# When ScalarE computes the next batch's sigmoids inside the tiles of the last feed-forward stage

## The reference

```python
    x = x + _L0_attn_ref(_L0_cond_ref(x, fside_BxSxS_0, fside_BxSxS_0, L0_cond_w, L0_cond_u, cond_512), ...)
    x = x + _L0_ffn_ref(_L0_cond2_ref(x, fside_BxSxS_0, ...), ...)      # routed experts
    x = x + _L1_attn_ref(_L1_cond_ref(x, fside_BxSxS_0, ...), ...)      # second layer: state-space block
    x = x + _L1_ffn_ref(_L1_cond2_ref(x, fside_BxSxS_0, ...), ...)      # second layer: feed-forward

        # in _L1_ffn_ref; _mx_linear quantises both of its operands in blocks of 32
        x2d = x.reshape(B * S, H)
        gate = _mx_linear(x2d, gate_w)
        up = _mx_linear(x2d, up_w)
        h = jax.nn.silu(gate) * up
        out = _mx_linear(h, down_w)
```

## Time and profile before

| | |
|---|---|
| median of 3 runs | 4275.18 us (4270.21 to 4276.04) |
| the profiled execution's own time | 4278.56 us |
| its span, first to last instruction | 4276.8 us |
| mean granted TensorE clock | 0.896 of full speed |
| TensorE busy | 3637.4 us, 85% of the span |
| VectorE busy | 2588.9 us, 61% |
| ScalarE busy | 1194.1 us, 28% |
| GpSimd busy | 558.0 us, 13% |

### The profile page before, as it was taken

One profiled execution on the slowest core, in us unless ns is written; L12 is line 12 of the kernel. 1 busy time (PEld: TensorE's weight loads), 2 busy tenths in 40 slices (PEclk: granted clock), 3 DMA queues, 4 the chain that ended last, 5 costly groups with the idle time before them and its releaser, 6 DMA issues.

```text
span 4276.8 us, 38855 instructions
## 1 busy us (share of the span) xinstructions
PE 3637.4 (85%) x13526; PEld 2272.7 (53%) x13526; DVE 2588.9 (61%) x3690; ACT 1194.1 (28%) x1974; POOL 558.0 (13%) x451
## 2 busy tenths in 40 slices
PE   2887887787879999998999779789979898889988
PEld 1653644545537777776776536543654356434743
DVE  5877877877845556776677344564346344644454
ACT  1332332323304444333333222212221222113210
POOL 1003002021021111110111112110212011201100
PEclk9989888889989999999999977899779887998799
DMA  3212202102117667666666510122013201221011
GB/s 142 60 31 61 68 18 74 55 18 72 38 33 258 211 230 236 219 229 197 230 220 226 187 74 30 69 103 79 30 55 117 79 30 54 74 105 48 1 59 40
DMA packets 277843, 444.62 MB, mean 104 GB/s; under 512 B 52560, under 2 KB 189776, under 8 KB 265104
## 3 DMA queue, kind: packets, MB, share of 16 engines
q1 hardware_dynamic: 256768, 383.74, 27.1%
q0 software_dynamic: 20880, 58.40, 4.3%
HBM read 368.49 MB, written 97.70 MB: 109 GB/s over the span
## 4 chain that ended last, share of the span: by engine, by line
PE 59%; DVE 20%; issue 9%; DVEq 5%; ACT 4%; DMA 2%; POOL 1%; POOLq 0%; SPq 0%; ACTq 0%
PE bank L964 14%; PE bank L975 7%; PE bank L1206 5%; PE bank L1219 5%; PE bank L1225 4%; PE bank L782 3%; PE bank L1073 3%; DVE sb_gla L1793 2%; DVE sb_ratio L1768 2%; DVEq L1774 2%; PE bank L1114 2%; PE bank L1092 1%; PE bank L759 1%; DVE sb_work L1805 1%; PE bank L762 1%
## 5 line engine op out<-in xcount | busy, mean ns | idle before, releaser
L964 PE MATMUL bank<-sb_xT,sb_work 128*128 128x256 f32 x3024 | 665.4, 380 | 1.6 <-issue 0.8
L964 PEld LDWEIGHTS bank<-sb_xT,sb_work 128*128 128x128 f32 x3024 | 576.0, 191 | 106.8 <-issue 31.3
L782 PE MATMUL bank<-sb_gla,sb_work 128*128 128x256 f32 x896 | 261.7, 445 | 111.7 <-DVE sb_work L1795 99.1
L975 PE MATMUL bank<-sb_work,sb_hT 128*128 128x512 f32 x756 | 351.0, 616 | 0.0
L1219 PE MATMUL bank<-sb_parts,sb_small 128*128 128x512 f32 x512 | 257.1, 649 | 43.8 <-ACT sb_work L1538 39.0
L782 PEld LDWEIGHTS bank<-sb_gla,sb_work 128*128 128x128 f32 x896 | 189.9, 219 | 174.8 <-DVE sb_work L1795 120.2
L762 PE MATMUL bank<-sb_hT,sb_work 128*128 128x512 f32 x384 | 180.5, 618 | 101.4 <-DVE sb_hT L1742 101.4
L1587 POOL DMA_INDIRECT sb_parts<-scratch_h,sb_small x126 | 136.0, 1079 | 983.3 <-DMA sb_small<-scratch_ids 963.8
L1073 PE MATMUL bank<-sb_parts,sb_hT 128*128 128x512 f32 x512 | 238.6, 627 | 0.0
L1206 PE MATMUL bank<-sb_work,sb_parts 128*128 128x512 f32 x512 | 233.5, 616 | 2.7 <-ACT sb_work L1544 2.7
L975 PEld LDWEIGHTS bank<-sb_work,sb_hT 128*128 128x128 f32 x756 | 145.9, 200 | 161.4 <-issue 161.4
(11 more groups left out here) (363 smaller groups left out, 6113.3 us busy)
## 6 DMA issues: line engine op xcount, KB each, us to landing
sb_work<-scratch_gu SPq DMA_DIRECT2D x63, 1408.0 KB, 7.5
sb_parts<-scratch_mx SPq DMA_DIRECT2D x16, 3072.0 KB, 10.4
sb_work<-moe_w SPq DMA_DIRECT2D x63, 512.0 KB, 5.1
scratch_y<-sb_work SPq DMA_DIRECT2D x63, 512.0 KB, 6.8
sb_parts<-scratch_fq SPq DMA_DIRECT2D x24, 1024.0 KB, 7.9
sb_work<-w_qkvg SPq DMA_DIRECT2D x64, 256.0 KB, 2.6
scratch_gu<-moe_w SPq DMA_DIRECT2D x32, 512.0 KB, 5.8
sb_parts<-fT SPq DMA_DIRECT2D x48, 256.0 KB, 3.7
```

The lines of the kernel that those rows point to most:

```text
L782: mm = pe.matmul(dst.rearrange("p (h n l) -> p h n l", h=HPC, l=size), kS[u % 2][:, k * P:(k + 1) * P], late[:, :, k, :, 1, :], start=True ...
L964: mm = pe.matmul(dst, egu[j % 3][:, which * NC + k, m * P:(m + 1) * P], xt[j % 2][:, k, :], start=(k == 0), stop=(k == NC - 1))
L975: mm = pe.matmul(bank(YB[s]), einter[j % 2][:, m * SLOTS + s * P:m * SLOTS + (s + 1) * P], edn[j % 3][:, m * D:(m + 1) * D], start=(m == 0 ...
```

## The change

In ScalarE's loop over the feed-forward tiles the call of `sigmoid2` moves from the start of the loop's body to its end. The sigmoid of tile `i` then stands behind the activation of tile `i` and behind the copy of tile `i - 1`, where it stood in front of both.

```diff
                 for i in range(FB * NT + 1):
-                    if b + 1 < NB and i >= 8 and i % 2 == 0 and i < 16:
-                        sigmoid2(b + 1, (i - 8) // 2)
                     if i < NT:
                         act.wait_ge(f_tq.sem, f_tq.at(b, i + 1))
...
                         act.activation(hqT[ib % 2][:, :, t * P:(t + 1) * P], r3(bank(6), P), ACT.Copy)\
                            .then_inc(f_hT.sem, 1)
+                    if b + 1 < NB and i >= 8 and i % 2 == 0 and i < 16:
+                        sigmoid2(b + 1, (i - 8) // 2)
```

## The result

| | before | after |
|---|---|---|
| median, four executions of each | 4273.01 us (4270.21 to 4276.04) | 4231.10 us (4221.36 to 4235.63) |
| ratio | | 0.9898, 95% interval 0.9886 to 0.9910 |
| profiled execution | 4278.56 us | 4230.84 us |
| its span | 4276.8 us | 4229.0 us |
| mean granted TensorE clock | 0.896 | 0.904 |

The change makes the kernel 1.0% faster, where 0.8% was forecast: 42 us between the medians and 47.7 us between the profiled executions, against a forecast of 33.3. The fourth execution of the kernel before moved its median from 4275.18 to 4273.01, which is 2.2 us of the 10.8 between the forecast of 4241.9 and the median; the other 8.6 are gain beyond the forecast. The part inside the feed-forward tiles came out as worked out. The rest comes from stretches in which no instruction differs.

The account below looks back on a forecast made before the run. TensorE, busy 85% of the span, was the engine to watch, standing still for late activations. Removed 54.3 us less added 21.0 gave 33.3; 4275.2 - 33.3 = 4241.9 us, range 4236 to 4257 to hold 8 of 10.

Parts of the forecast that it names:

- What goes: Gate products of tiles 9 and 13, six places: activation waits of 40.0 us and slow restarts of 14.3 removed, together 54.3.
- What comes late next: VectorE delays TensorE's up products and transposes at tiles 9 and 13: new waits add 21.0 us in all.
- What the moved sigmoid costs: At its new place behind the copy of tile i - 1: cost 0, upper end 2.4 us.
- The clock at the new waits: TensorE's new waits at tiles 9 and 13: clock fall taken as 0 per place, bounds 0 and 2.97 us.
- The first rival: Clock falls at the six places' new waits all the same: gain 22.3 us, time 4253, upper bound 4260; chance 0.17.
- The rule of the Trainium skill: Short idle times between matmul groups let the clock go down and up; each of the places would keep a slow restart.
- What follows in the batch: Tiles 14 and 15 and the next batch's weights keep their distances and only come earlier, with no further gain.

Follow-up runs that it names:

- even_only: Kernel before with only the sigmoids of tiles 8 and 12 moved to the end of the tile: 4230.28 us, ratio 0.9897.
- odd_only: Kernel before with only the sigmoids of tiles 10 and 14 moved: 4273.36 us beside 4273.47, ratio 1.0001.
- the delays: Transposes of tile 13 done three times over: in the kernel before 4270.12 us, ratio 0.9990; in the changed kernel 4240.93 us, ratio 0.9925.
- the fastest kernel: Changed kernel with VectorE's weighted sums in tiles 4, 5, 8, 9, sigmoids paired, and matmuls of constants filling TensorE's waits: 4190.10 us, ratio 0.9797.

## Why the prediction was right about the change and wrong about the kernel

**What goes** held. The wait for the activation was removed at six places with the slow restart behind it, and even_only and odd_only show that tiles 8 and 12 alone account for it.

**What comes late next** held, with small errors. Tile 9: recorded waits of 1.01 and 1.95 us for 1.36 and 2.00 forecast; tile 13: 1.30 and 1.73 for 1.65 and 2.00. The recorded waits leave out the modelled end of the group before; counted from start to start as in the forecast they are 1.18, 2.22, 1.47 and 2.00, 6.87 us for 7.01. My step of 0.09 us from the sum to the product was wrong: the product started 0.09 us ahead of the sum's recorded end. The sum over the tiles, 33.8 us for 33.3, is right to 2%. One row was misread, with no effect on the sum: 2808.91 is the start of the sigmoid's table load, not its end, which is 2810.19.

**What the moved sigmoid costs**: nothing, as forecast (odd_only, 1.0001).

**The clock at the new waits** held at all six places. After waits of 0.95 to 1.96 us TensorE was not slowed: up products of 3.70 us, transposes of 0.66 us and down products of 13.9. The first rival, a fall at each of the six places, did not occur. That these waits were short enough was a choice between 0 and 2.97 us, with no row to decide it: the choice came true, it was not worked out. The rule of the Trainium skill that the prediction set against it, from "TensorE: Matmul & The Clock Gate", section "A second HAM failure mode: psum-queue depth-cycling", did not hold at these waits between full products; in the state-space stage it does.

**The step that failed** is in the sum: "What follows in the batch (...) keeps its distances and only comes earlier." That put a term at zero. What follows came earlier and was also shorter, by 13.9 us in the profiled execution: 10.7 in the state-space stages of batches 1 to 3 and 3.5 between the last down products and the next batch, less 0.3 elsewhere. I had a wait of 2.67 us before me that lowers the clock, and slow restarts of 5.34 to 6.58 us after waits of nearly one length (6.36 to 6.71 us), which show that the price of a wait is not fixed by its length. I gave the effect some 5 us on either side of zero. The stages above put it at 210.3 to 224.2 us for one batch's state-space stage, so at up to 14 us per batch. My estimate from that is that the range should have been about twice as wide on both sides.

That the sign was a gain here was not to be had from the trace of before. By the delays, another 0.87 us per batch takes 10 us of the gain back. So of the 42 to 48 us measured, 34 belong to the change and the rest, a piece of luck, to where it happened to put the later waits. This last is shown by the trace for the profiled executions; for the medians it is inferred, since only one execution of each kernel has a trace. What decides where in the stage the clock falls stays open.

## What to carry to other kernels

On an engine that works in order, put what waits for another engine behind what others wait for; look for the first instruction behind each long wait and ask who needs it. Then follow the chain to the engine that is late next, and place its side work in tiles in which the bounding engine has a long piece of its own: that was worth another 20 us in the tiles here. Where a profile has stages in which TensorE's clock falls at short waits, treat their length as a range and not as a number, judge a change by the stretch it touches, and test a small gain with a small added delay before trusting it.

## What was not expected of the hardware

- After a wait of 2.67 us line 1035 runs at the lower clock for a part in one kernel (12.26 us) and not in another (10.68 us after 2.66 us), with the same instructions on both sides. With 0.87 us of added work ahead of it the short one became long in all three batches (12.27 to 12.37 us), the long one short in one batch of three.
- One stage with equal instructions and, to 0.01 us, equal busy times of all other engines takes 210.3 and 224.2 us in one execution, at a mean granted clock of 0.87 and 0.81. In batch 0, with nothing different ahead of it, it takes 217.2 to 223.7 us from execution to execution.
- A delay of 3.5 us in all made the kernel before 0.1% faster (0.9982 to 0.9999), and cost the fastest kernel 19 us by the medians.
- Matmuls of constants, which compute nothing of use, save 0.5% of the kernel's time (0.9937 to 0.9967); 17 us of it, 0.4%, show in the trace where they keep the clock up, around waits of 5.8 and 2.7 us.
